# An eight-head attention layer in a four-layer graph network: the order of its first head's work

## The reference

```python
h = (x @ W).reshape(n, heads, out_c)                 # 625 x 8 x 96
al_s = jnp.einsum('nhc,hc->nh', h, a_src)
al_d = jnp.einsum('nhc,hc->nh', h, a_dst)
e = jax.nn.leaky_relu(al_s[src] + al_d[dst], 0.2)
m = jax.ops.segment_max(e, dst, num_segments=n)
ex = jnp.exp(e - m[dst])
z = jax.ops.segment_sum(ex, dst, num_segments=n)
out = segment_sum(h[src] * (ex / (z[dst] + 1e-16))[:, :, None], dst) + bias
```

## Time and profile before

| what | value |
|---|---|
| median of 3 runs | 1421.93 us (1421.38 to 1422.33) |
| the profiled execution | 1422.3 us |
| its span, first to last instruction | 1420.6 us |
| mean granted clock of TensorE | 0.994 of full speed |
| PE busy in the span | 1358.8 us (96%) |
| DVE, ACT, POOL busy | 773.7, 446.5, 550.3 us |

### The profile page before, as it was taken

How to read it: one execution, slowest core, us unless ns; L and a number is a source line. 1 busy time by engine, 2 the same in 40 slices (tenths; PEclk the granted TensorE clock), 3 DMA queues, 4 the chain that set the end, 5 groups by cost and what they waited for, 6 DMA issues and landing times.

```text
span 1420.6 us, 22617 instructions
## 1 busy us (share of the span) xinstructions
PE 1358.8 (96%) x7834; PEld 1280.5 (90%) x7834; DVE 773.7 (54%) x1826; ACT 446.5 (31%) x937; POOL 550.3 (39%) x628
## 2 busy tenths in 40 slices
PE   5999999999999999999999999999998999988997
PEld 3676999999999999999999999999887987778897
DVE  6876755223545256465232344657356363589656
ACT  1564522111110000100010132154466333458832
POOL 8000324325234524353424242323345472566830
PEclk9999999999999999999999999999999999999999
DMA  3101111212434133233212131222111320210001
GB/s 118 55 30 35 39 34 44 57 34 86 122 99 124 56 89 108 77 116 102 67 34 62 40 89 34 52 67 81 43 29 50 100 72 12 67 51 1 1 1 55
DMA packets 57803, 86.49 MB, mean 61 GB/s; under 512 B 6467, under 2 KB 54458, under 8 KB 57583
## 3 DMA queue, kind: packets, MB, share of 16 engines
q1 hardware_dynamic: 45204, 65.82, 15.8%
q10 hardware_dynamic: 12504, 19.36, 4.4%
HBM read 83.24 MB, written 1.92 MB: 60 GB/s over the span
## 4 chain that ended last, share of the span: by engine, by line
PE 79%; DVE 10%; ACT 4%; POOL 3%; issue 3%; DMA 1%; DVEq 0%; SPq 0%; ACTq 0%; POOLq 0%
PE psum L2583 13%; PE psum L2586 13%; PE psum L2587 13%; PE psum L2600 8%; PE psum L2603 7%; PE psum L3084 3%; PE psum L2732 2%; DVE max_scratch L2276 2%; PE psum L2657 2%; PE psum L2996 1%; PE psum L2626 1%; PE psum L2629 1%; PE psum L3000 1%; PE psum L3001 1%; PE psum L2572 1%
## 5 line engine op out<-in xcount | busy, mean ns | idle before, releaser
L2583 PE MATMUL psum<-w_lo,xT_hi 128*125 128x384 f32 (+4 forms) x1110 | 378.0, 341 | 3.4 <-POOL w_lo L929 1.6
L2586 PE MATMUL psum<-w_hi,xT_lo 128*125 128x384 f32 (+4 forms) x1110 | 374.0, 337 | 0.0
L2587 PE MATMUL psum<-w_hi,xT_hi 128*125 128x384 f32 (+4 forms) x1110 | 374.0, 337 | 0.0
L916 POOL CAST w_hi<-w_raw 128x384 fp32r<-128x384 f32 x190 | 105.2, 553 | 569.3 <-PE psum L2587 465.9
L1104 ACT ACTIVATE h_hi<-psum 125x384 fp32r<-125x384 f32 (+1 forms) x120 | 59.1, 492 | 529.3 <-PE psum L2587 524.9
L1794 DVE TENSOR_TENSOR h_lo<-psum,h_hi 125x384 fp32r<-125x384 f32 (+1 forms) x120 | 66.9, 558 | 286.7 <-ACT h_hi L1104 285.9
L2583 PEld LDWEIGHTS psum<-w_lo,xT_hi 128*125 128x125 f32 (+1 forms) x1110 | 206.4, 186 | 6.2 <-POOL w_lo L929 3.4
L2586 PEld LDWEIGHTS psum<-w_hi,xT_lo 128*125 128x125 f32 (+1 forms) x1110 | 206.8, 186 | 0.4
L918 POOL TENSOR_TENSOR w_lo<-w_raw,w_hi 128x384 fp32r<-128x384 f32 x190 | 201.2, 1059 | 15.2
L2587 PEld LDWEIGHTS psum<-w_hi,xT_hi 128*125 128x125 f32 (+1 forms) x1110 | 206.6, 186 | 0.0
L2600 PE MATMUL psum<-h_lo,adjacency 125*125 125x384 f32 (+3 forms) x600 | 203.5, 339 | 2.1 <-issue 1.9
(11 more groups left out here) (364 smaller groups left out, 2313.0 us busy)
## 6 DMA issues: line engine op xcount, KB each, us to landing
w_raw<-weights_dram SPq DMA_DIRECT2D x296, 192.0 KB, 2.4
score_w_raw<-weights_dram ACTq DMA_DIRECT2D x58, 192.0 KB, 2.8
x_nat<-x_dram SPq DMA_DIRECT2D x1, 1875.0 KB
x_residual<-x_dram SPq DMA_DIRECT2D x5, 375.0 KB
score_a_rows<-L_gnn_a_src_dram ACTq DMA_DIRECT2D x8, 192.0 KB, 3.4
score_a_rows<-L_gnn_a_dst_dram ACTq DMA_DIRECT2D x8, 192.0 KB, 4.7
out_dram<-x_residual SPq DMA_DIRECT2D x4, 375.0 KB
rgcn_bias<-rgcn_bias_dram SPq DMA_DIRECT2D x1, 1125.0 KB
```

The lines of the kernel that those rows point to most:

```text
L916: nc.gpsimd.tensor_copy(mem.wh[:, slot, :], mem.raw[:, raw_slot, :]).then_inc(w_hi_ready, 1)
L2583: ins = nc.tensor.matmul(o, h, wl, start=(j == 0), stop=False, skip_group_check=True)
L2586: nc.tensor.matmul(o, l, wh, start=False, stop=False, skip_group_check=True)
L2587: ins = nc.tensor.matmul(o, h, wh, start=False, stop=stop and j == k - 1, skip_group_check=True)
```

## The change

Seven edits, all of them in Q2:

1. `chunks_and_scores` sends three of six chunks block by block for the eight-head layer, not two.
2. `HEAD_EVENTS`: row 0 ahead of unit 4 (it was 5), row 1 of unit 12 (14), row 2 of unit 20 (23), columns of head 0 of unit 21 (26).
3. DVE makes the maxima of heads 0 and 1 one after the other, and then the columns of both heads at once.
4. For head 0 DVE makes all five score tiles before it multiplies the first two by the counts. Other heads keep their order.
5. ACT takes head 0's exponentials for tiles 0 to 2 between the copies of the second piece's blocks 2 to 4, and those of tiles 3 and 4 behind them. They all came behind these copies.
6. ACT takes an exponential of one element ahead of the second piece's copies, with which the function's table is loaded, and copies head 0's flat column one block earlier.
7. At the start of the second piece's copies ACT makes high halves up to chunk 18, not up to chunk 19.

POOL's and SP's programs are as they were.

```diff
-HEAD_EVENTS = {2: (("scores", 0),), 5: (("row", 0),), 14: (("row", 1),), 23: (("row", 2),), 26: (("send", 0),)}
+HEAD_EVENTS = {2: (("scores", 0),), 4: (("row", 0),), 12: (("row", 1),), 20: (("row", 2),), 21: (("send", 0),)}
...
+            def first_exps(k):
+
+                if k < NB - LATE:
+                    source_exp(Q2, 0, k)
+                else:
+                    source_below(0, k)
+                    source_exp_below(0, k)
+
...
                     if m == 0 and piece:
-                        split_hi(q.chunk + (piece + 1) * q.k + 8)
+                        split_hi(q.chunk + (piece + 1) * q.k + (7 if q is Q2 else 8))
+                        if q is Q2:
+                            nc.scalar.activation(mem.elu[0:1, 0, 0, 0:1], mem.ones[0:1, 0:1], ACT.Exp)
+                    if piece and q is Q2 and m >= 2:
+                        first_exps(m - 2)
...
-                    elif piece == 1 and q is Q2 and m == 2:
+                    elif piece == 1 and q is Q2 and m == 1:
                         keep_flat(q, 0)
...
-            head_exps(0)
+            for k in range(3, NB):
+                first_exps(k)
...
-                for k in range(NB):
-                    if k == NB - LATE + 1:
-                        if h % 2:
-                            columns(Q2, h + 1, min(h + 3, HEADS3))
-                        for i in range(NB - LATE):
-                            finish(Q2, h, i)
+                at = NB - LATE + 1 if h else NB
+                for k in range(at):
                     score(Q2, h, k)
-
-            scores_of(Q2, 0)
-            scores_of(Q2, 1)
+                if h % 2:
+                    columns(Q2, h + 1, min(h + 3, HEADS3))
+                for k in range(NB - LATE):
+                    finish(Q2, h, k)
+                for k in range(at, NB):
+                    score(Q2, h, k)
+
+            maxima(Q2, 0)
+            maxima(Q2, 1)
+            columns(Q2, 0, 2)
...
-                p, whole = 0, q.k - 2
+                p, whole = 0, q.k - (3 if q.by_head else 2)
```

## The result

The changed kernel takes 1437.99 us (median of 5, 1434.94 to 1438.08) against 1421.93 us: a ratio of 1.0106 (of the means), 95% interval 1.0092 to 1.012. It is slower by 16.1 us; the forecast was 12 us slower, 1434 us, with a range of 1431.5 to 1437. The profiled execution took 1438.08 us, its span is 1436.4 us (before 1420.6), the mean granted clock 0.986 (before 0.994). It is the longest of the five. The two shortest, 1434.94 and 1436.13 us, have a mean granted clock of 0.988 against 0.983 to 0.986 in the other three, but only the longest was profiled.

The account below looks back on a forecast made before the run. PE was taken as busy for 96% of the span, with head 0's sum in Q2 shifting all that follows. S at 1276.7 plus 16.7 gave T 1293.4 against 1281.6, +11.8 us: 1434 us against 1421.93, range 1431.5 to 1437.

Parts of the forecast that it names:

- the stop: In Q2 POOL waits some 24 us for chunk 19's high half, holding back head 0's sum; S to T 16.7 us.
- the single terms from S to POOL's last product: ACT's last tiles 2.2, high to low half 0.60, low half 0.97, casts 2.09, biases 5.5, late products 4.06 us.
- S: End of head 1's scores on DVE in Q2: predicted at 1276.7 us against 1281.55, 4.8 us earlier.
- T: Moment head 0's sum is done and DVE can go on: predicted 1293.4 us against 1281.6, +11.8 us.
- What the change takes off: Walk down DVE's list in Q2 with earlier durations: head 1's scores end 4.8 us earlier, at 1276.7 us.
- Its reason for the columns: Joint columns of heads 0 and 1 on DVE cost 0.56 us, since POOL is idle; 2.60 was the other end.
- Its reason for the products by counts: Head 0's two products on DVE take 1.45 us without the 1.41 us wait, since ACT's exponentials come in time.
- the last ten of fifty passes on PE, 6.08 / 5, and a handover of 0.1: 1.3: Last term from S to T: end of head 0's sum on PE behind POOL's late products, 1.3 us.
- full speed would take off 0.1 us: Claim that slow PE passes enter only the last term up to T, where the full clock would save 0.1 us.
- After T nothing is given back: Behind head 0's sum DVE, then ACT, have no slack, so the whole +11.8 us stays to the end.
- the slow clock stays: Rival: PE stays at 1.2 GHz for one or two heads behind T, 1435 to 1437 us; chance 0.10.
- The fast one: Rival: POOL isn't held at chunk 19, T would be S, 1276.8, 4.8 us earlier: 1417 us; chance 0.06.

Follow-up runs that it names:

- e2: Kernel before, with only ACT's high halves at the second piece's start cut to chunk 18: 1441.17 us, ratio 1.0137.
- e1: Changed kernel, but POOL makes low halves only up to chunk 18 ahead of its casts: 1421.07 us, ratio 0.9992.
- e7: e6 with POOL's casts ahead of Q2's low halves and its biases waiting for DVE's joint columns: 1417.36 us, ratio 0.9966.
- e9: e7, but DVE multiplies head 0's first two tiles by the counts behind the third score, as before: 1418.82 us.
- e4: Changed kernel with 110 and 22 extra PE matmuls, ahead of POOL's first bias and the late products: 1443.47 us.
- e4b: Changed kernel with 64 and 13 extra PE matmuls at the same places as e4: 1435.1 us, ratio 1.0091.
- e6: e1 with 10, 5 and 5 extra PE matmuls ahead of the columns of heads 2, 4 and 6: 1418.43 us, ratio 0.9977.
- e5: Changed kernel, but ACT makes chunk 19's high half right behind its copy of the second piece's last block: 1427.7 us, ratio 1.0041.
- e11: e7, but DVE makes head 0's columns right behind head 0's maxima and head 1's behind head 1's: 1419.73 us, ratio 0.9984.

## Why the prediction was right about the stop and too low

**The stop: right.** POOL's 24 us, ended by ACT's high half near 1279, PE's idle time of 15 us (though its bracket names no POOL bias, only "issue"), and the single terms from S to POOL's last product (2.2, 0.58, 0.94, 2.12, 5.32, 4.01 us) came as worked out, 15.17 against 15.4. DVE's idle time was 19.04 us and not 16.5; the difference is the failed step below. e2 makes the loss with edit 7 alone, and e1 takes the wait for T away by taking POOL's stop away.

**What the change takes off: right.** A leg of 30.11 us from the first maximum to S against 30.0 by the walk (1276.7 - 1246.7). Its reason for the columns, an idle POOL, is what e1 and e7 measured from the other side. Its reason for the products by counts, that ACT is in time, held too, with POOL idle beside them (1.52 us, no wait). With POOL at work it is not the whole: e9 shows that there edit 4's place keeps them away from POOL's biases. That S came 0.78 us earlier than forecast is luck: 0.92 us of its shift is PE's later second piece in the execution of before, and S hid 0.8 us of the miss that follows.

**The step that failed is a size: "the last ten of fifty passes on PE, 6.08 / 5, and a handover of 0.1: 1.3".** It measured 3.87. The 6.08 us of the earlier trace rows were passes that began at the slow clock behind a hole of 5.25 us and were soon at the full one, as the busy times of before show:

```profile
1275.64:1276.64 1.00, 1.00 (x7) 1.00 (x7) 1.00 (x2) 0.17 (x1) 0.00 (x0) 0.50 0.00 0
1276.64:1277.64 1.00, 1.00 (x11) 1.00 (x10) 1.00 (x2) 1.00 (x2) 0.00 (x0) 0.95 0.00 0
```

Dividing them by five gave 0.12 us for each pass, nearly the full-speed price (0.115 in e4). Behind a hole of 15.42 us, with twenty slow passes and a wait of 1.15 us in between, they cost 0.217 each, and not ten but thirty of them lag behind POOL: thirty times 0.217 is 6.5 us, longer than POOL's last two products. The prediction had the hole and the slow level in its text and took "full speed would take off 0.1 us" from the wrong row; the earlier trace rows had the right ratio too, columns at 4.53 against 2.18. e4b takes the slow clock away and gets 16.58 for the predicted 16.7.

**"After T nothing is given back": too little.** Nothing was given back, and 1.26 us were lost at head 6's columns. That is not the rival "the slow clock stays": behind T the clock was 1.00, and head 2's columns took 2.44 us, so that the 0.3 us which the prediction allowed for them did not come either. The clock fell anew, 20 us later (head 4, without cost) and 40 us later (head 6). The prediction argued that the stretch of 40.8 us ran at 1.00; it did, but with holes of 1.87 and 2.49 us ahead of the columns of heads 4 and 6, which the trace showed, and behind which the clock can fall. The 1.22 us of the last write were outside any step. Of the 4.0 us by which the profiled execution missed the sum, the passes make 2.6 and these two 2.5; 1.0 went the other way, most of it the luck with S.

**The rivals.** The fast one was worked out for T alone. Without the stop T came 0.5 us from where it said, and the kernel still took 1421.07 us: PE's wait had moved behind head 0's sum, which cost 1.9 us, and the end came 1.7 us later, which is open. It took e6 and e7 to make it 1417.36.

The Trainium skill, SBUF — State Buffer, Who interferes with whom, says that a DVE instruction with two inputs in SBUF contends with a POOL instruction that reads SBUF, and one with a single SBUF input, outside its two-port performance modes, doesn't; the prediction had the rule without these conditions. The runs agree on both halves: products by counts at 1.97 to 2.11 us against 0.80 beside POOL in e5, score tiles with one input in PSUM unchanged at 1.63 for two.

## What to carry to other kernels

When a producer's step is moved back in one engine's list, look at every list that demands its result in order: here one high half that no product needed before the last layer held back the biases and products that stood behind its low half. Price PE's work behind a new hole at the clock that the trace shows behind an old one, over all passes that lag and not only the last few; a hole that is removed in one place may come up in another, as e1's 3.19 us did, and cheap extra matmuls in it can pay (e6). When DVE's work moves, see what POOL does at the new place.

## What the hardware did that was not expected

The same hole of 2.5 us ahead of the same columns was followed by the full clock before (2.42 us), and by the slow one in the changed kernel (3.97), in e1 (3.42) and in e4b (4.53): the price of a short hole does not follow from its length alone. The Trainium skill, TensorE: Matmul & The Clock Gate, Part 1, says that the chip's measure of activity runs free of the kernel's start, so that the place where the clock changes differs from one execution to the next. The two groups of e11's times could come from it; that it is the cause no run here shows. And small DVE instructions of 0.17 us took up to 1.33 us beside POOL (e5; 1.07 in e11), many times their own length.
